# A two-layer transformer block on one Trainium2 core: the last group of experts gathers its partner rows plainly and ahead of the results of group three, and VectorE adds them

## What is computed

```python
def moe_apply(x, combine, dispatch, W, b):
    disp = jnp.einsum('sec,sd->ecd', dispatch, x)
    h = jnp.einsum('ecd,edf->ecf', disp, W) + b[:, None, :]
    return jnp.einsum('sec,ecf->sf', combine, h)

def per_group(xf, lw, lb):                       # four groups of 1024 tokens
    combine, dispatch = top2_dispatch(xf, Wg, C) # 24 experts, two for each token, C = 86
    h = moe_apply(xf, combine, dispatch, W1, b1) # 128 -> 512
    h = layer_norm(h, lw, lb)
    h = jax.nn.relu(h)
    return moe_apply(h, combine, dispatch, W2, b2)  # 512 -> 128
...
return layer_norm(out + x, ln_out_w, ln_out_b)
x = x + _layernorm(_L1_ffn_ref(_layernorm(x, axis=-1), ...), axis=-1)
```

## Time and profile before

| | us |
|---|---|
| median of 3 executions | 1141.59 (1141.51 to 1143.92) |
| the profiled execution | 1136.46 |
| its span in the trace | 1134.7 |
| busy: TensorE (products) | 899.2 |
| busy: ScalarE | 783.2 |
| busy: VectorE | 595.0 |
| busy: GpSimd | 361.0 |
| first partner gather of the last group starts | 1030.72 |
| last `result` of the last group starts | 1094.83 |

### The profile page before, as it was taken

The page is one execution under the profiler, slowest core; times in us unless marked ns, Lnnn a source line. Parts: engine busy times, 40 slices in busy tenths (PEclk is TensorE's granted clock), DMA queues, the critical chain, the costliest instruction groups (busy, mean ns, idle before and its releaser), DMA issues. The chain is left out here.

```text
span 1134.7 us, 19198 instructions
## 1 busy us (share of the span) xinstructions
PE 899.2 (79%) x6570; PEld 421.6 (37%) x6570; DVE 595.0 (52%) x2000; ACT 783.2 (69%) x1188; POOL 361.0 (32%) x332
## 2 busy tenths in 40 slices
PE   3757983673879999999989999998869888686650
PEld 3644761331112222222222223232347566455650
DVE  7489867895001444444454235333353236686557
ACT  1235351455979999999989999996566665675530
POOL 5322432555200000000000000213586577765743
PEclk9767996886989999999999999999979998898875
DMA  3000002457921211121211112245786755677841
GB/s 104 1 1 1 1 1 62 91 128 164 301 59 44 60 33 52 42 61 42 61 39 34 55 43 62 58 122 159 239 147 153 224 161 163 190 227 145 164 118 53
DMA packets 91258, 109.67 MB, mean 97 GB/s; under 512 B 11997, under 2 KB 62814, under 8 KB 91050
## 3 DMA queue, kind: packets, MB, share of 16 engines
q1 hardware_dynamic: 77320, 80.00, 24.2%
q0 software_dynamic: 12416, 27.80, 11.7%
q10 hardware_dynamic: 1442, 0.86, 0.3%
HBM read 68.90 MB, written 39.71 MB: 96 GB/s over the span
## 5 line engine op out<-in xcount | busy, mean ns | idle before, releaser
L1510 ACT ACTIVATE s_e<-s_ps 128x1024 f32<-128x1024 f32 x512 | 477.0, 1067 | 20.5 <-PE s_ps L1680 19.8
L1693 PE MATMUL s_acc<-s_e,s_v 128*32 128x512 f32 x2048 | 276.3, 612 | 0.7 <-ACT s_e L1510 0.7
L1127 POOL DMA_INDIRECT x_in<-x_tokens,rows_of x72 | 74.1, 1029 | 463.6 <-DVE rows_of L1286 427.7
L1680 PE MATMUL s_ps<-qk 51*128 51x512 bf16 x1024 | 181.3, 391 | 32.2 <-ACT s_e L1510 9.8
L1680 PEld LDWEIGHTS s_ps<-qk 51*128 51x128 bf16 x1024 | 41.1, 94 | 282.4 <-ACT s_e L1510 254.1
L2031 PE MATMUL e_py<-w,qk 128*96 128x128 f32 x768 | 106.9, 289 | 0.0
L2119 ACT ACTIVATE qk<-e_pn,ln_hid 128x288 f32<-128x288 f32 x192 | 85.8, 505 | 29.9 <-PE e_pn L2015 29.9
L2031 PEld LDWEIGHTS e_py<-w,qk 128*96 128x96 f32 x768 | 96.3, 176 | 0.0
L2001 PE MATMUL e_ph<-w,qk 128*32 128x512 f32 x576 | 78.4, 617 | 8.9 <-ACT e_hs L2086 5.9
L1127 POOL DMA_INDIRECT e_ya<-y_rows,take x64 | 65.5, 1024 | 34.7 <-issue 28.6
L2015 PE MATMUL e_pn<-ident,e_hs 128*128 128x128 f32 x216 | 40.6, 306 | 44.5 <-ACT qk L2119 23.3
(11 more groups left out here) (429 smaller groups left out, 1430.8 us busy)
## 6 DMA issues: line engine op xcount, KB each, us to landing
h_rows<-e_hs SPq DMA_DIRECT2D x54, 256.0 KB, 3.7
qk<-parts_q SPq DMA_DIRECT2D x64, 96.0 KB
qk<-parts_k SPq DMA_DIRECT2D x64, 96.0 KB
w<-in_w SPq DMA_DIRECT2D x1, 6144.0 KB, 21.0
h_rows<-x_res SPq DMA_DIRECT2D x18, 256.0 KB, 2.4
qk<-parts_k SPq DMA_DIRECT2D x64, 64.0 KB
parts_q<-b_parts SPq DMA_DIRECT2D x16, 192.0 KB, 2.7
parts_k<-b_parts SPq DMA_DIRECT2D x16, 192.0 KB, 2.8
```

The costliest lines, as they stand in the source:

```text
L1127: nc.gpsimd.indirect_dma_start(dst, None, rows, bass.IndirectOffsetOnAxis(ap=idx, axis=0), compute_op=op).then_inc(R["landed"][k % FLIGHT] ...
L1510: nc.scalar.activation(E[g % 4][:, 2 * pair:2 * pair + 2, :], pS[BUFFER["score", 2 * g + pair]][:].rearrange("p (a s) -> p a s", a=2), ACT ...
L1680: last = nc.tensor.matmul(pS[BUFFER["score", 2 * g + pair]][:, a * CH:(a + 1) * CH], K[c % 2][rows, pair, j * P:(j + 1) * P], Q[c % 2][row ...
L1693: last = nc.tensor.matmul(acc[hu % 2][32 * h:32 * h + 32, :], V4[c % 2][:, j, h, :], E[g % 4][:, h, :], start=j == 0, stop=j == TB - 1)
```

## The change

In the last group `partners_added` is no longer used. GpSimd issues all 18 partner gathers plainly, and the 16 result gathers of group three, which stood between them and behind them, follow. VectorE adds the partner rows, so `added` has no early return for the last group and ScalarE's `square` waits for the addition. Since VectorE's order is rewritten there, `summed(1, 1)` and `output(1, 1)` move: from ahead of the last group to behind `result(18)`, and from behind `normed(19)` to behind `result(19)`. On SyncE, `x_store(1, 1)` and `x_load(2, 1)` move from behind the store of unit 19 to behind that of unit 21, and the last group's loads wait for all additions.

```diff
 STAGES:
-          "h18 h19 h20 h21 y16 y17 h22 y18 y19 h23 y20 y21 ... y31").split()
+          "h18 h19 h20 h21 h22 h23 y16 y17 y18 y19 y20 y21 ... y31").split()
 x_load:
                 if h == GR - 1:
-                    sp.wait_ge(add_done, (GR - 2) * NT)
+                    sp.wait_ge(add_done, (GR - 1) * NT)
 SyncE, over the units (h = m // NB, j = m % NB):
-                if h >= 2 and 1 <= j <= 2:
-                    x_load(h - 1, j - 1)
+                if (h, j) in ((2, 1), (2, 2), (3, 1), (3, 4)):
+                    x_load(h - 1, int(j > 1))
...
-                if h >= 2 and j < 2:
-                    x_store(h - 2, j)
+                if (h, j) in ((2, 0), (2, 1), (3, 0), (3, 3)):
+                    x_store(h - 2, int(j > 0))
 GpSimd:
             results(12, 16)
-            partners_added(18, 22)
-            results(16, 18)
-            partners_added(22, 23)
-            results(18, 20)
-            partners_added(23, 24)
+            partners(18, 24)
+            results(16, 20)
             results(20, 24)
 ScalarE, square:
-                if t // NT in (0, GR - 1):
+                if t < NT:
                     landed(act, R, place("h", t // NT, t % NT))
                 else:
                     act.wait_ge(add_done, t - NT + 1)
 VectorE, added:
-                if m // NB == GR - 1:
-                    return
 VectorE, the loop now over groups 1 and 2, in group 2:
-                if h == 2:
-                    summed(1, 1)
                 result(m + 4)
-                if h < GR - 1:
-                    added(m + 6)
+                added(m + 6)
                 result(m + 5)
 VectorE, the last group written out:
+            m = (GR - 1) * NB
+            added(m + 1)
+            normed(m)
+            added(m + 2)
+            normed(m + 1)
+            added(m + 3)
+            normed(m + 2)
+            result(m)
+            summed(1, 1)
+            added(m + 4)
+            normed(m + 3)
+            result(m + 1)
+            output(1, 1)
+            added(m + 5)
+            normed(m + 4)
+            result(m + 2)
+            normed(m + 5)
+            result(m + 3)
+            collected(2, 0)
+            summed(2, 0)
+            result(m + 4)
+            collected(2, 1)
+            result(m + 5)
```

More of the change, by code:

```diff
@@ L1106 @@
           "h12 h13 x22 h14 x23 h15 y8 y9 h16 y10 y11 h17 y12 y13 y14 y15 "
-          "h18 h19 h20 h21 y16 y17 h22 y18 y19 h23 y20 y21 y22 y23 y24 y25 y26 y27 y28 y29 y30 y31").split()
+          "h18 h19 h20 h21 h22 h23 y16 y17 y18 y19 y20 y21 y22 y23 y24 y25 y26 y27 y28 y29 y30 y31").split()
 LENGTH = {"x": TPB, "h": TPB, "y": 2}
@@ L2260, in _ @@
             v.wait_ge(w_in, 16)
-            for h in range(1, GR):
+            for h in range(1, GR - 1):
                 m = h * NB
@@ L2269, in _ @@
                     summed(0, 1)
-                if h == 3:
-                    output(1, 1)
                 added(m + 3)
@@ L2281, in _ @@
                 normed(m + 4)
-                if h >= 2:
-                    collected(h - 1, 0)
-                    summed(h - 1, 0)
+                if h == 2:
+                    collected(1, 0)
+                    summed(1, 0)
                 result(m + 2)
@@ L2294, in _ @@
                     output(0, 0)
-                if h >= 2:
-                    collected(h - 1, 1)
                 if h == 2:
-                    summed(1, 1)
+                    collected(1, 1)
                 result(m + 4)
-                if h < GR - 1:
-                    added(m + 6)
+                added(m + 6)
                 result(m + 5)
+            m = (GR - 1) * NB
[21 more added lines that the diff above has]
+            result(m + 5)
             output(2, 0)
```

## The result

| | before | after |
|---|---|---|
| median of 5 executions each, us | 1143.74 (1141.51 to 1144.96) | 1137.71 (1134.99 to 1139.24) |
| the profiled execution, us | 1136.46 | 1139.24 |
| its span, us | 1134.7 | 1137.5 |
| first partner gather of the last group starts (S) | 1030.72 | 1038.24 |
| `result(23)` starts | 1094.83 | 1097.61 |

The ratio is 0.9954, with an interval of 0.9934 to 0.9974: 5.3 us faster, between 3.0 and 7.6 (the two medians as they stand differ by 6.0). The forecast was -2.6 us; it gave a chance of 0.46 to a kernel faster by more than 0.2%.

What follows compares the result with a forecast made beforehand. It took the last group's chain through gathers as the bound, then VectorE's 17.4 us and the loads; `result(23)` at 1092.2 against 1094.8 gave -2.6, carried to the end: 1141.6 - 2.6 = 1139.0 us, range 1137.0 to 1144.0.

Steps and rivals of the forecast that it cites:

- Step 1: Last group's first six gathers, plain with four buffers: sixth add starts 11.05 us after the first gather, ends at 1042.46.
- rival of slow landings: Four-buffer gather loop paced by landings up to 6.7 us: +2.7, 1144.3 us; chance 0.17, plus 0.05 with slow loads.
- Step 2: Unit 18 of the last group: first relu at 1044.8 instead of 1047.20, 2.4 us gained; its last product ends at 1053.6.
- Step 3: VectorE from `result(18)` to the add freeing unit 23: 17.4 us of unhidden own work; `result(21)` at 1081.7, 4.0 us ahead.
- Step 4: SyncE's moved `x_store(1, 1)` and `x_load(2, 1)` hold `result(23)`: 10.5 us behind `result(21)`, at 1092.2 against 1094.8.
- loads don't hold: Stores and loads land sooner, only TensorE's 9.13 us counts: `result(23)` at 1090.8, -4.0, 1137.6 us; chance 0.13.
- Step 5: Group three's result gathers (near 1062 to 1082), VectorE's other additions and the order table of landings: cost nothing.
- the tail: From `result(23)` to the end, GpSimd fetching sixteen results and VectorE finishing groups three and four: 39.9 us, carried over unchanged.
- what would show it: List of expected trace signs in the last group, from unit 18's first relu near 1044.8 to `result(23)` near 1092.

Runs made afterwards that it cites:

- repeat of after: The changed kernel measured once more, unaltered, on another chip than its first measurement: ratio 0.9975, 1138.81 us.
- summed early: The changed kernel with `summed(1, 1)` put back ahead of the last group: ratio 0.9947, 1137.84 us.
- adding, reordered: Kernel before with all partner gathers first, still adding in the DMA, and `collected(2, 0)`, `summed(2, 0)`, `collected(2, 1)` moved later on VectorE: ratio 0.9955, 1136.69 us.
- plain, interleaved: The changed kernel with gathers in the order of before, result gathers between partner gathers, still plain and added by VectorE: ratio 0.9937, 1136.21 us.
- adding gathers first: Kernel before with only the gather order changed: all 18 partner gathers first, still adding in the DMA, VectorE's order kept: ratio 1.0022, 1144.55 us.
- the fourth kernel: The changed kernel with `output(1, 1)` alone moved, behind `normed(22)`, and `x_store(1, 1)` behind unit 20's store; run only on the slow chip: ratio 1.0047.

## Why the prediction was right, and where it was not

The side was right and the size was half: -2.6 forecast, -4.7 in the stage, -5.3 (3.0 to 7.6) in the ratio. The repeat of after gave less, -2.9 in the ratio. The five steps, in us after S, from the first profile of after:

- **Step 1, six gathers.** Sixth addition ends at 12.1, forecast 11.7. The sixth gather starts at 6.8, forecast 6.9. First landings were quicker than at 960 (first addition at 3.3, not 4.2), and the seventh gather took 1.60 instead of 0.94 us beside two additions, as at 1005 in the earlier trace rows. By the Trainium skill ("SBUF — State Buffer", section "SBUF: two separate sides"), a VectorE instruction with two SBUF inputs takes the shared ports against a GpSimd instruction that reads SBUF, and the later of the two blocks fully. The seventh gather agrees in direction. The sixth doesn't: it took 0.94 with an addition (1045.18, 0.69 us) beside it from start to end, and most gathers of the loop took 0.94 to 1.2. The rival of slow landings did not come: no addition of unit 18 or 19 waited over 1.8 us.
- **Step 2, unit 18.** First relu at 14.5, forecast 14.1; `result(18)` at 23.05, forecast 22.9. Right.
- **Step 3, the chain.** Output ends at 40.3, as forecast; the square starts at 41.0, forecast 41.1. VectorE's 17.4 us were right to a tenth. Two statements beside them were not. That "each us more there is a us at the end" is refuted by summed early, where 5.33 us less gave 0.6; only with the output out of the chain as well did the end follow. And of the gathers 13 to 18, said to wait for VectorE, 13 to 16 followed each other after the usual 0.30 us; only the seventeenth did, 7.52 us. From square to `result(21)` it took 8.86 us, not 9.85. That 1.0 us was luck: in the repeat of after, with its squares as close together, it took 9.86. What differs is how soon TensorE was back at the 2.4 GHz level (last section).
- **Step 4, the loads.** From `result(21)` to `result(23)` 9.54 us, not 10.5. The step failed in what it named as the holder. SyncE of after, output stores, first load and last load:

```profile
1089.13 1.02 SPq L1849 DMA_DIRECT2D out_x<-v_all  x2
1092.20 0.37 SPq L1859 DMA_DIRECT2D v_all<-x_tokens  x1
...
1093.65 0.47 SPq L1861 DMA_DIRECT2D v_all<-x_rows  x1
```

  Store to load was 3.07 us, under every row, and the last load landed within 2.6 us of its start, in time. What set the 9.54 was VectorE's own queue, which I had not added up there: `result(21)` 0.6, `collected(2, 0)` 1.4, `summed(2, 0)` 5.3, `result(22)` 0.7, `collected(2, 1)` 1.4, together 9.4, just over TensorE's 9.13. The rival "loads don't hold" had the mechanism half right (-4.0): the loads didn't hold it, but VectorE did, and not TensorE. In the repeat, 9.56 us, the loads held it by 0.24 us, so the two are nearly level. The loads of the earlier trace rows had run beside a DMA share of 0.87 (1000 to 1005) and 0.75 (1069 to 1075), the second farther from full than the forecast put it.
- **Step 5 and the tail.** The tail is 39.9 as carried over. The sixteen result gathers ran from 32.6 to 53.9 (forecast 31 to 51), hidden, as said.

The two terms that came out short are 1.0 us each, and the square came 0.1 sooner than forecast: together the 2.1 us between -2.6 and -4.7. Only the second, step 4, is a fault of the sum that showed twice; its 10.5 measured 9.54 and 9.56. One reading of the trace before was wrong too, though no term hangs on it: TensorE was granted 1.00 already in 1055 to 1062, not 0.99 "only behind 1083". Of the "what would show it" list, only "idle before `collected(2, 1)`, ended by the loads" was not seen in the first profile.

What the prediction didn't see is what the change is made of. It took the plain form for the source of the gain and VectorE's chain for its price. The runs show that the plain form and the gather order are each replaceable (adding, reordered and plain, interleaved: the same gain), and that the gather order alone gives nothing while VectorE's order stands. Adding, reordered differs from adding gathers first in VectorE's order alone, and its `result(23)` comes 8.4 us sooner: there VectorE's order is shown to make the gain. With the gathers in their old order and adding, it was not run. With plain gathers, the better order for VectorE gave 1132.69 us.

Open: why the second measurement of after gave half the gain of the first in ratio (its stage lost only 0.8 us, less than the 1.0 that step 3 puts down to TensorE's clock); why the stage of before took 1.5 us more the second time; what the fourth kernel is worth alone; what moves S by several us between executions.

## What to carry to other kernels

When work moves to an engine that executes in order, add up everything queued between the two points that others wait for, on that engine, before asking about transfers: here it was right for 17.4 us and was left out for the last 9.4. An order of gathers is worth what the reader's own order lets it be worth: moved alone, it turned 7.6 us of earlier data into a 10.5 us stand at the next reader. Put the last work on earlier groups behind the last step that frees another engine: with the output there, the kernel gave its best time. Ahead of the first step of a ring of buffers such work has a price too: 5.3 us of it held the sixth addition up by 2.4. And run the unchanged program twice before believing a difference of under 2 us in one stage.

## What was not expected of the hardware

- The start of the last group varied from 1030.72 to 1036.75 us between two executions of the kernel before, more than the change is worth, and was 1038.24 and 1034.16 in two of after, which does the same work up to there, but for `summed(1, 1)`. Two profiles can be compared only from a common event on.
- On one chip every kernel took about 5% longer, with stops of ScalarE of 10 to 15 us whose end the trace puts down to no instruction or transfer of the core, while GpSimd went on.
- TensorE's return to 2.4 GHz behind a stand. In after it stood still for 5.57 us before the second relu of unit 21 let it go on. TensorE, the transposes behind that and three chunks:

```profile
1080.79 0.90 PE L2012 MATMUL e_pn<-ident,e_hs 128*128 128x128 f32 x3 [5.57 <-ACT qk L2116]
...
1081.90 1.97 PE L2028 MATMUL e_py<-w,qk 128*96 128x128 f32 x8
...
1084.31 1.32 PE L2028 MATMUL e_py<-w,qk 128*96 128x128 f32 x8
...
1085.79 1.04 PE L2028 MATMUL e_py<-w,qk 128*96 128x128 f32 x8
```

  The same chunk (eight products) took 1.97, 1.32, 1.04 us, and in the kernel before, behind a stand of 3.79 us, 1.96, 1.91, 1.04. In the repeat of after the stand was 4.42 us:

```profile
1077.60 1.97 PE L2028 MATMUL e_py<-w,qk 128*96 128x128 f32 x8
...
1080.00 1.91 PE L2028 MATMUL e_py<-w,qk 128*96 128x128 f32 x8
...
1082.34 1.18 PE L2028 MATMUL e_py<-w,qk 128*96 128x128 f32 x8
```

  The longer times are the 1.2 GHz level. The first profile of after is granted 0.53 in 1078 to 1079, ahead of TensorE's next work at 1080.79, 0.56 in 1084 to 1085 and 1.00 in 1085 to 1086. The repeat is granted 0.90 in 1075 to 1076, just ahead of its next work at 1076.47, 0.69 in 1082 to 1083 and 1.00 in 1083 to 1084. So more of the slow stretch fell into the stand in the first, and less of it on products. That is the 1.0 us between 8.86 and 9.86 in step 3, in one and the same program. No run varied it alone.
